# Attention with experts on one core: early squares shared with GpSimd, early pieces shared with ScalarE

## The reference, cut to what matters

```python
def attn(x):                                  # 16 heads of 8 channels
    s = q @ k.T                               # per head, 1024 x 1024
    s = s - s.mean(-1); mad = abs(s).mean(-1) + 1e-6
    s = s / mad * score_gain
    r = max(where(causal, s, -1000), 0) ** 4
    return (r / (r.sum(-1) + 1e-6)) @ v @ W_proj + b_proj
def ffn(x):                                   # 8 experts, top 2
    z = (x @ w1[e] + b1[e]) * (x @ w2[e] + b2[e])
    return sum_e we * (silu(z @ wg[e] + bg[e]) @ w3[e] + b3[e])
out = x + attn(xn) + ffn(xn)
```

## Time and profile before

| | |
|---|---|
| median of 3 runs | 805.56 us (805.55 to 853.74) |
| the profiled execution | 808.65 us, its span 806.9 us |
| TensorE busy | 735.7 us (91%) |
| VectorE busy | 671.1 us (83%) |
| ScalarE busy | 675.7 us (84%) |
| GpSimd busy | 513.7 us (64%) |
| mean granted TensorE clock | 0.96 |

### The profile page before, as it was taken

One profiled execution on the slowest core, in us unless ns is written; L12 is line 12 of the kernel. 1 busy time (PEld: TensorE's weight loads), 2 busy tenths in 40 slices (PEclk: granted clock), 3 DMA queues, 4 the chain that ended last, 5 costly groups with the idle time before them and its releaser, 6 DMA issues.

```text
span 806.9 us, 17975 instructions
## 1 busy us (share of the span) xinstructions
PE 735.7 (91%) x5850; PEld 336.0 (42%) x5853; DVE 671.1 (83%) x1866; ACT 675.7 (84%) x1527; POOL 513.7 (64%) x537
## 2 busy tenths in 40 slices
PE   7978888889999999999999999999999999999886
PEld 6622121214444445444444444444444445443224
DVE  7679999998978887887888879788877988888883
ACT  4768989898888897988889898888989888898880
POOL 4015666745867667595766759576675957669690
PEclk9986889999999999999999999999999999999899
DMA  8865122274514542351334335133422623321395
GB/s 249 287 211 211 38 72 61 76 203 104 119 53 132 137 113 54 102 140 45 104 107 121 108 108 137 40 108 104 114 78 85 170 82 95 97 58 30 78 141 129
DMA packets 58350, 90.87 MB, mean 113 GB/s; under 512 B 8960, under 2 KB 41344, under 8 KB 58256
## 3 DMA queue, kind: packets, MB, share of 16 engines
q1 hardware_dynamic: 43200, 75.21, 33.7%
q0 software_dynamic: 10784, 12.53, 7.0%
q10 hardware_dynamic: 4272, 1.98, 0.8%
HBM read 61.29 MB, written 28.06 MB: 111 GB/s over the span
## 4 chain that ended last, share of the span: by engine, by line
PE 45%; DVE 24%; ACT 13%; issue 10%; POOL 7%; DMA 1%; DVEq 0%; ACTq 0%; SPq 0%; POOLq 0%
PE bank L983 17%; DVE W L1329 12%; PE bank L1018 7%; DVE junk_V L1321 6%; PE bank L998 6%; PE bank L1059 4%; ACT U L835 4%; POOL W L681 4%; ACT junk_A L827 3%; PE bank L1023 3%; PE bank L1068 3%; ACT W L856 2%; DVE W L1333 2%; PE bank L907 1%; ACT U L838 1%
## 5 line engine op out<-in xcount | busy, mean ns | idle before, releaser
L1329 DVE SCALAR_TENSOR_TENSOR W<-bank,U 128x512 f32<-128x512 f32 (+1 forms) x512 | 300.6, 649 | 21.4 <-ACT U L835 19.6
L983 PE MATMUL bank<-W,VS 128*10 128x512 f32 (+3 forms) x1536 | 297.5, 508 | 13.2 <-ACT W L856 9.0
L983 PE MATMUL bank<-U,usel 128*10 128x512 f32 (+3 forms) x1536 | 294.0, 506 | 0.0
L835 ACT ACTIVATE U<-bank 128x512 f32<-128x512 f32 (+1 forms) x512 | 253.9, 599 | 19.7 <-PE bank L1068 18.3
L1321 DVE TENSOR_SCALAR_CACHE_REDUCE junk_V<-bank 128x512 bf16<-128x512 f32 (+3 forms) x445 | 218.4, 533 | 55.7 <-PE bank L1059 54.9
L681 POOL TENSOR_TENSOR W<-W 128x1024 f32<-128x1024 f32 (+2 forms) x159 | 233.9, 1481 | 13.7 <-DVE W L1329 4.0
L670 POOL TENSOR_SCALAR_AFFINE_SELECT W<-W 128x512 f32<-128x512 f32 x127 | 83.0, 654 | 176.5 <-DVE W L1329 89.9
L856 ACT ACTIVATE W<-W 128x256 f32<-128x256 f32 (+2 forms) x225 | 192.2, 881 | 2.2 <-POOL W L670 1.2
L1068 PE MATMUL bank<-QS,KS 48*128 48x512 bf16 (+3 forms) x768 | 148.8, 334 | 19.8 <-DVE W L1329 12.9
L827 ACT ACTIVATE junk_A<-bank 128x512 bf16<-128x512 f32 (+3 forms) x195 | 88.2, 461 | 48.3 <-PE bank L1059 48.0
L1059 PE MATMUL bank<-KS,QS 48*128 48x512 bf16 (+3 forms) x640 | 98.8, 325 | 3.1 <-DVE parts L1265 1.7
(11 more groups left out here) (166 smaller groups left out, 673.2 us busy)
## 6 DMA issues: line engine op xcount, KB each, us to landing
wb<-in_experts SPq DMA_DIRECT2D x39, 707.0 KB, 5.5
qk_parts<-parts SPq DMA_DIRECT2D x8, 768.0 KB, 5.6
KS<-qk_parts SPq DMA_DIRECT2D x192, 32.0 KB
QS<-qk_parts SPq DMA_DIRECT2D x192, 32.0 KB
xt_all<-sorted_x SPq DMA_DIRECT2D x39, 130.0 KB, 5.9
sorted_x<-xt_all SPq DMA_DIRECT2D x3, 1300.0 KB, 12.0
xn_row<-weighted_y POOLq DMA_DIRECT2D x6, 512.0 KB, 7.1
v_stationary<-vb SPq DMA_DIRECT2D x4, 640.0 KB, 4.3
```

What stands on the lines that cost most here:

```text
L835: act.activation(U[n % NU][:, g, 0:w], score(n, k), ACT.Relu).then_inc(u_ready, 1)
L983: last = pe.matmul(acc[32 * g:32 * g + VW, lo:HALF], usel[:, :] if of_u else VS[q % 2][:, j, :, g], (U if of_u else W)[n % NU][:, g, 0:HAL ...
L1329: vec.scalar_tensor_tensor(W[n % NU][:, g, 0:w], score(n, k), 0.0, U[n % NU][:, g, 0:w], ALU.max, ALU.mult).then_inc(w_done, 1)
```

## The change

Two things change, both in the first three quads. GpSimd takes one of the two squares (p = 1, two heads, 128x1024) of each full unit, units 4 to 7 of a quad, while the scatters run: 12 squares in all leave ScalarE. And of the 28 pieces of a quad six go from VectorE to ScalarE: one in unit 2, two in unit 3, one in unit 10, two in unit 11, so 18 in the three quads. Nothing is changed from unit 36 on, and nothing is computed otherwise.

```diff
-    plan = lambda n: PLAN[n % NS].replace("A", "V") if n < EARLY * NS else PLAN[n % NS]
+    PLAN_EARLY = ["VV", "VVV", "VAV", "VAVA", "V", "V", "V", "V", "VV", "VVV", "VAV", "VAVA"]
+    plan = lambda n: PLAN_EARLY[n % NS] if n < EARLY * NS else PLAN[n % NS]
```

```diff
     POOL_SQUARES = [(1,), (1,), (1,), (1,), (0,), (0,), (0,), (0, 1), (), (1,), (1,), (1,)]
-    by_pool = lambda n, p: n * PER_STEP >= SCATTERS and p in POOL_SQUARES[n % NS]
+    by_pool = lambda n, p: p in POOL_SQUARES[n % NS] if n * PER_STEP >= SCATTERS else n % NS in (4, 5, 6, 7) and p == 1
```

## The result

The changed kernel takes 811.87 us (median of 4 executions, 810.57 to 812.77) against 805.55 us before; the ratio is 1.0073 (95% interval 1.0059 to 1.0087). It is 6.3 us slower, where +1.4 was forecast. The time lies in the range (802 to 813 us), near its upper end, and within 2%. (One execution of the kernel before, 853.74 us, was in the chip's slower state and doesn't count in the ratio.) The profiled execution of after took 810.57 us with a span of 808.8, only 1.9 more than that of before.

What follows compares the result with a forecast made beforehand. VectorE and ScalarE bound the early units, TensorE the later ones; after the change GpSimd would pace the early quads. Terms 0.4 + 2.0 - 1.0 = +1.4 us on the median of 805.56 gave 807.0 us, range 802 to 813.

Steps and rivals of the forecast that it cites:

- the price of the clock: Rival: TensorE's clock falls once more in each quad's full units, 3 x 1.7 = 5.1 us, some 812 us; chance 0.25.
- the tokens' delay: Rival: GpSimd 4 us later than forecast, SyncE's load lands late, first transposition waits about 2 us: 809 us; chance 0.05.
- the walk: GpSimd's timeline from unit 3 to 31 without waits: mask of unit 20 3.0 us late, square of unit 31 ending at 177.4.
- The rival with 2.22 us for a square: GpSimd's twelve squares, at the Trainium skill's price, cost 4 us more: 811 us; chance 0.02.
- The bound: First three quads: GpSimd needs 41.8 us a quad, as a quad took before, so VectorE's and ScalarE's savings aren't harvested.
- The rival in which GpSimd doesn't bind: First three quads: a quad takes 39.2 us, in all 7.8 us less, 797.8 us; chance 0.08.
- First term: At unit 31's average: GpSimd's square ends at 177.4, where ScalarE's pair of squares ended at 177.0 before: +0.4 us.
- Second term: GpSimd's waits, as masks of wide units need VectorE's W: between 0 and 2.6 us, taken as +2.0.
- Third term: Units 32 to 35: GpSimd is free, VectorE has three pieces less: between 0 and -2.1 us, taken as -1.0.
- The pieces on ScalarE: Six pieces gained, four squares lost: net +0.5, ScalarE at 38.3 us a quad; alone, a quad near 39.2 us.
- The signs: Wrong if second quad under 40.5 us, GpSimd waits over 5 us for VectorE, or low-clock stretches grow over one a quad.

Runs made afterwards that it cites:

- after_again: The changed kernel, nothing altered, run and traced once more beside the kernel before on one chip: 811.54 us, ratio 1.0063.
- before_again: The kernel before, nothing altered, run and traced once more beside the changed kernel on one chip: 806.35 us.

## Why the prediction was right or wrong

**The number.** The time is in the range, and this is in part luck. The upper end, 813 us, was made of the price of the clock and of half of the tokens' delay, and neither was paid. What the kernel lost beyond the forecast came from GpSimd's waits, for which 2.6 us had been the most, from 0.8 us in the walk, and from 1.0 us in the trace that stood for the kernel before. The rival with 2.22 us for a square names 811 us, close to what was measured, and that price wasn't paid either.

**The bound.** Right. GpSimd, 64% busy on the page, became the pace of the early units, at 4.36 us a full unit (4.32 forecast) and 3.07 a masked one (3.06). A quad's relief for VectorE was not harvested. The second quad, from the mask of unit 12 to that of unit 24, took 44.8 and 45.6 us in the two traces after, against 41.8 in both before. The rival in which GpSimd doesn't bind is refuted for four squares, and is what happens with two.

The 0.30 us behind a scatter stand only ahead of another scatter: a mask behind one begins without them, 0.98 us after its start (112.87 to 113.85). They come once a unit, as the sums have it.

**First term, the walk without waits (+0.4).** Right in its parts. Told from the mask of unit 0, the square of unit 31 should have ended at 177.4 - 64.6 = 112.8 us. The mask of unit 3 came 0.5 us later than in the walk (73.80 - 63.53 = 10.3, not 9.8), and the squares and the rewriting took 0.3 more. But the other side of the difference, the kernel before, was read from a trace that ran about 1.0 us slower in this stretch than the second one (its mask of unit 8 at 28.6 behind unit 0, against 27.6). The first term should have been +1.4 for that alone.

**Second term, GpSimd's waits (+2.0).** This is the step that failed, by its size. They measured 4.5 us in after_again, nine waits from unit 4 to unit 28, and 3.6 us in the first trace after, eight waits; even the upper bound had been 2.6. I had counted the masks of units 1 and 9 of a quad, at 0.64. Those of unit 1 waited 0.66. Those of unit 9 in fact waited for nothing: right behind the full units GpSimd was late itself. What I had not counted were the masks of units 0, 3 and 11 of a quad and the square of its unit 4. The masks of unit 3 stood with 1.23 and 1.18 us of idle time in the rows that I had read the earlier trace rows; I had taken it for slack. From after_again:

```profile
77.33 1.89 POOL L682 TENSOR_TENSOR W<-W 128x1024 f32<-128x1024 f32 x1 [0.49 <-DVE W L1330]
...
107.35 0.63 POOL L671 TENSOR_SCALAR_AFFINE_SELECT W<-W 128x512 f32<-128x512 f32 x1 [0.38 <-DVE W L1330]
...
117.71 0.63 POOL L671 TENSOR_SCALAR_AFFINE_SELECT W<-W 128x512 f32<-128x512 f32 x1 [0.58 <-DVE W L1334]
...
152.98 0.63 POOL L671 TENSOR_SCALAR_AFFINE_SELECT W<-W 128x512 f32<-128x512 f32 x1 [0.58 <-DVE W L1330]
```

They all lie around the turn of a half or a quad, where the units go from 128 columns back to 512. My reading is that GpSimd has by then made up its lateness and asks again for a W that isn't there. An engine at the edge of being the bound loses twice: it paces the others, and each time that the work they owe it comes late it loses what it can't make up.

**Third term, units 32 to 35 (-1.0).** Right. At the square of unit 31 (181.51 in after_again; ScalarE's pair in before_again ended at 174.98) the changed kernel stood 6.5 us behind, at the mask of unit 36 5.7.

Together: 1.0 of the reference, 0.5 and 0.3 of the walk, 2.5 of the waits and 0.2 of the third term are 4.5 us; with the forecast's 1.4 that is 5.9, and 5.7 was measured. This account is made after the fact, from one pair of traces.

**The pieces on ScalarE.** I had priced them and the four squares together, at 38.3 us of ScalarE a quad and 39.2 us for the quad. That case can't be run as it stands, since the squares must be done somewhere. Its nearest is the run with two squares a quad, where GpSimd doesn't bind: by the same rows ScalarE needs 38.3 + 2 x 0.95 = 40.2 us, and a third of the stage is 123.09 / 3 = 41.0, or 40.6 in the first trace. Of the 0.9 us of air that I gave it, 0.8 and 0.4 were there, if ScalarE is the bound. What I didn't say is that with all four squares left on it ScalarE is the bound at once, which the run with the pieces alone showed.

**The tokens.** Right in that they stayed hidden. In after_again SyncE's load was issued at 180.91 and TensorE came for the tokens at 186.8, with 2.4 us to landing: 3.5 us of slack left, where 1.6 plus TensorE's own 1.4 had been forecast. Both sides were later than in the walk: the load by 9.4 us against before_again (5.4 forecast for the last scatter), TensorE by 5.7 (1.4). No wait of the early units is put down to a load of SyncE.

**The clock.** As far as the traces go, the rival's price was not paid: 0.7 us lie between the two traces of the changed kernel. Read in steps of 1 us, the granted clock stood at 0.50 in eight stretches of the stage in both of them, and in six in both traces of before, so less than one more a quad.

**The signs.** The waits stayed under the 5 us that would have told me wrong. But two of the places that I named were missed, told from the mask of unit 0 in each trace: the mask of unit 20 came 5.9 to 7.1 us later than before (some 3 forecast), that of unit 32 5.5 to 7.2 us later (3 at most). The last scatter began at 177.5 and 178.6, not near 175. So the loss was on its way by unit 20.

**The price of a square.** The square took 1.90 us, as in the trace of before, not the estimate of 2.22 from the Trainium skill, "GPSIMD Engine Reference", section 3.1 (Elementwise). Its rule, VectorE for elementwise work, can't be judged by this case: four squares a quad were a loss, but for a reason that isn't in the price, what stands in the queue behind them, and with two a quad the kernel gained a little.

## What to carry to other kernels

Before giving an idle engine more, add up its own timeline over a period of the loop, with its gaps, and hold the sum against the period: the stretch showed 28.75 us busy in 41.8; with the gaps the work needed 8 x 3.06 + 4 x 2.6 = 34.9 us, and 41.8 with four squares. Half of the squares fitted where all of them did not. Where such a sum comes out at the period itself, expect a loss: the engine's own waits come on top of it (3.6 and 4.5 us here). A move of work between three engines is best tried in its parts and in doses: both parts alone were losses here, both together too, and half of one with the whole of the other was a small gain.

## What the runs showed that was not expected

A product on GpSimd that nobody waits for cost 4.4 us of the whole kernel, by standing ahead of masks. The part behind unit 36 took 616.1 to 617.5 us in 14 traces of ten programs. A single profiled execution can stand 3 us off its kernel's median (808.65 against 805.56), half of what was to be found here. And one chip ran the kernel before 14 us slower than the others did, but its variants at 811 to 818 us; a comparison made there alone would have called every one of them a gain, even the scatters dealt otherwise, which were 7.9 us slower than the kernel before on another chip.
